# A vision tower of state-space tokens, gated scan and mixture of experts on one core: feature products over 128 rows, with their operands regrouped by transfers on the chip

## The reference

```python
K   = 2 * Re( sum_n Ct[c,h,n] * exp(dA_log[h,n] * l) )      # 16 x 256 x 512: the tokens
h   = concat(cls_tok, K)                                     # 16 x 257 x 512
u   = layernorm(layernorm(h)) * gamma + beta
a, b, c = split(u @ W_in + b_in);  s_t = (1 - sig(a)) s_{t-1} + sig(a) b
h  += (s * tanh(c)) @ W_out + b_out + layernorm(h) @ W_skip + b_skip
x   = layernorm(h)
h  += sum over the 2 best of 8 experts: score * (silu(x Wg) * (x Wu)) Wd
    + (silu(x Sg) * (x Su)) Sd                               # shared expert
```

## Time and profile before

| what | value |
|---|---|
| three runs | 1191.7, 1199.46 (median), 1201.67 us |
| profiled execution | 1196.48 us, its span 1194.8 us |
| mean granted TensorE clock | 0.944 of full |
| PE, DVE, ACT, POOL busy | 1059.5, 812.2, 347.2, 383.9 us (89, 68, 29, 32% of the span) |
| first stage, rounds 3 to 14 | 192.60 to 663.72 us |
| expert stage | from about 773 us |

### The profile page before, as it was taken

One profiled execution on the slowest core, in us unless ns is written; L12 is line 12 of the kernel. 1 busy time (PEld: TensorE's weight loads), 2 busy tenths in 40 slices (PEclk: granted clock), 3 DMA queues, 4 the chain that ended last, 5 costly groups with the idle time before them and its releaser, 6 DMA issues.

```text
span 1194.8 us, 26490 instructions
## 1 busy us (share of the span) xinstructions
PE 1059.5 (89%) x7869; PEld 696.9 (58%) x7870; DVE 812.2 (68%) x2123; ACT 347.2 (29%) x658; POOL 383.9 (32%) x352
## 2 busy tenths in 40 slices
PE   3046898999999999999999994989999999999995
PEld 3034566666766676667766771655555555555552
DVE  7976988898889888988898563544444444444442
ACT  4413433443344333443344332111111111111110
POOL 1011221222123211332022210145545656655554
PEclk8556998999999999999999997899999999999998
DMA  7322456455545555455535589689998777877885
GB/s 247 112 53 54 105 159 154 124 152 173 149 127 150 170 151 143 139 171 162 165 112 157 170 258 371 188 170 217 224 172 132 130 130 130 134 132 128 133 124 74
DMA packets 311150, 183.57 MB, mean 154 GB/s; under 512 B 261218, under 2 KB 280034, under 8 KB 309044
## 3 DMA queue, kind: packets, MB, share of 16 engines
q1 hardware_dynamic: 292948, 135.83, 46.8%
q0 software_dynamic: 15504, 36.46, 15.2%
q10 hardware_dynamic: 2640, 10.54, 2.3%
HBM read 53.40 MB, written 79.73 MB: 111 GB/s over the span
## 4 chain that ended last, share of the span: by engine, by line
PE 75%; DVE 3%; SPq 3%; DMA 3%; issue 2%; ACT 1%; POOLq 0%; POOL 0%; ACTq 0%; DVEq 0%
PE bank L997 30%; PE bank L1146 10%; PE bank L1156 10%; PE bank L1147 10%; PE bank L1072 8%; PE bank L1011 4%; DMA out<-x2w,rows_in 2%; SPq L779 1%; SPq L781 1%; PE bank L1076 1%; ACT tokens L1202 1%; PE bank L1062 1%; DMA wexp<-w_halves 1%; PE bank L1075 1%; DVE wexp L1351 0%
## 5 line engine op out<-in xcount | busy, mean ns | idle before, releaser
L997 PE MATMUL bank<-wexp 128*128 128x256 f16 (+2 forms) x3252 | 418.6, 291 | 24.8 <-issue 9.5
L997 PEld LDWEIGHTS bank<-wexp 128*128 128x128 f16 x3252 | 316.4, 101 | 110.7 <-issue 33.7
L1146 PE MATMUL bank<-wexp,rows_in 128*128 x852 | 255.5, 313 | 9.6 <-issue 6.9
L1147 PE MATMUL bank<-wexp,rows_in 128*128 x852 | 255.1, 312 | 0.0
L975 POOL DMA_INDIRECT out<-x2w,rows_in x71 | 113.7, 1601 | 116.0 <-DMA out<-x2w,rows_in 82.8
L927 POOL TENSOR_TENSOR inv<-var,power 128x4 f32<-128x4 f32 x17 | 29.2, 1717 | 375.0 <-DVE var L1533 375.0
L1689 DVE SCALAR_TENSOR_TENSOR mixed<-bank,mixed 128x352 f32<-128x352 f32 x71 | 37.2, 525 | 161.0 <-ACT mixed L1308 108.4
L963 POOL TENSOR_TENSOR ex<-base,ld 128x8 f32<-128x8 f32 x71 | 120.7, 1699 | 75.9 <-DVE ld L1668 56.0
L1146 PEld LDWEIGHTS bank<-wexp,rows_in 128*128 128x128 f16 x852 | 83.1, 98 | 66.6 <-issue 25.9
L1308 ACT ACTIVATE mixed<-bank 128x352 f32<-128x352 f32 x71 | 32.9, 464 | 295.3 <-PE bank L1147 295.3
L1156 PE MATMUL bank<-wexp,gates 128*128 (+1 forms) x477 | 111.7, 379 | 2.9 <-DVE x2w L1684 2.9
(11 more groups left out here) (281 smaller groups left out, 1247.3 us busy)
## 6 DMA issues: line engine op xcount, KB each, us to landing
w_halves<-rows_in SPq DMA_DIRECT2D x16, 704.0 KB
wexp<-w_halves ACTq DMA_DIRECT2D x1, 8704.0 KB
...
h_tok<-tokens SPq DMA_DIRECT2D x16, 512.0 KB, 2.7
...
```

The lines of the kernel that those rows point to most:

```text
L997: last = MM(dst, stat_of(step, a), mov_of(step, b), start=(s_ == 0 and a + b == 0), stop=(s_ == len(steps) - 1 and a == 1))
L1146: MM(GB[:, 0:H], xT[b][:, a, c, :], wexp[:, u, o:o + H], start=s_, stop=e_)
L1147: last = MM(UB[:, 0:H], xT[b][:, a, c, :], wexp[:, u, o + H:o + 2 * H], start=s_, stop=e_)
```

## The change

1. **Features.** After `tok_e` and after `tok_p`, SP copies the operands inside SBUF (`regroup`): half `f` of partition block `t` goes to partition block `f` of index `t`. `ea` goes to `et`, `pp` to `pt`, four DMAs each. PE then makes one product over all 128 partitions per `t` and `j`: 16 per chunk. `et` and `pt` are so read by PE, and `tok_e` part 0 waits for the previous feature products.
2. **Order on DVE.** `tok_e` for chunk k+2 moves from the end of body k-1 into body k, between the gate products; `tok_p` 1 to 5 stand around the second `project_out`, ahead of both `rows_lo` and both `down_out`.
3. **Banks.** The features use the banks of `shared_down` (3 and 0) instead of 1 and 2; PE waits for `c_dev` (`down_out`) instead of `c_gm` ahead of them, and for `c_toke` only ahead of the third gate product group.
4. **End of the first stage.** `pads_d` rows become whole rows (2112 bytes): SP writes their zeros at the end of body 1, and `pad_rows` is one copy from DRAM to DRAM per expert. Expert 4's copy stands ahead of the second x3 transpose of body 16. ACT's weight DMA is issued at the start of body 15. In the expert stage SP loads a unit at every third tile instead of every second.
5. **First rounds.** PE makes products whose result nobody reads (`idle_products`): 36 in body -1, 10 and 28 in body 0.

```diff
@@ -807,6 +807,12 @@
                     row = sp.value_load(tbl[0:1, 1, bass.ds(i, 1)], min_val=0, max_val=NR - P)
                     sp.dma_start_transpose(xT[b][:].rearrange("p h k t -> p (h k) t"), xs_d[bass.ds(row, P), 0:2 * D]).then_inc(d_xl[b], 16)
                     sp.dma_start(ext[b][:].bitcast(I32), xs_d[bass.ds(row, P), 2 * D:XW].bitcast(I32)).then_inc(d_xl[b], 16)
+
+                def regroup(to, of, sem):
+
+                    for t in range(2):
+                        for f in range(2):
+                            sp.dma_start(to[f * N:(f + 1) * N, t], of[t * N:(t + 1) * N, f]).then_inc(sem, 16)
 
                 def body(k, q):
                     if htok(k + 1):
@@ -819,6 +825,11 @@
                             sp.dma_start(hx[:, i, :].rearrange("p (b a) -> p b a", a=NA), src[:, i]).then_inc(c_hx, 16)
                     elif k + 1 == 0:
                         sp.dma_start(hx[:, 0, :], cls_tok.rearrange("a b d -> (a b) d").broadcast_to([P, D])).then_inc(c_hx, 32)
+                    if isinstance(k, int) and k == -1:
+                        sp.wait_ge(c_eap, 1)
+                        regroup(et, ea, c_ste)
+                        sp.wait_ge(c_tokp, 1)
+                        regroup(pt, pp, c_stp)
                     if htok(k - 1):
                         sp.wait_ge(c_wl, k - 1)
                         store_unit(k - 2)
...
                             load(b, b)
+                    if htok(k + 2) and not (isinstance(k, int) and k == -1):
+                        sp.wait_ge(c_eap, k + 2)
+                        regroup(et, ea, c_ste)
                     if has(k + 1):
                         n = k + 1
                         sp.wait_ge(c_lo2, n + 1)
@@ -853,13 +867,17 @@
                         at_least(sp, c_rt, n)
                         apart(sp, c_sps)
                         for i in range(tiles(n)):
+                            if i == 1 and isinstance(k, int) and k == NCH:
+                                pad_rows(sp, 4)
+                            if i == tiles(n) - 1 and htok(k + 2):
+                                sp.wait_ge(c_tokp, k + 2)
+                                regroup(pt, pp, c_stp)
                             sp.wait_ge(c_lo3, n * 2 + (i + 1) * 2 // tiles(n))
                             apart(sp, c_sps)
                             sp.dma_start_transpose(x3T[:, i].rearrange("p h k t -> p (h k) t"),
                                                    x3w[:, i, 0:2 * D]).then_inc(c_e3[i], 16)
                     if isinstance(k, int) and k == NCH:
-                        for e in range(4, 6):
-                            pad_rows(sp, e)
+                        pad_rows(sp, 5)
                     if has(k - 1):
...
                         sp.dma_start(dst, hst[:].rearrange("p j t a -> p (j t a)")).then_inc(c_hst, 16)
+                    if isinstance(k, int) and k == 1:
+                        for r in range(4):
+                            sp.dma_start(pads_d[:, r, :, 0:2 * D].bitcast(I32).rearrange("e q w -> q e w"),
+                                         zrow[:, 0:2 * D].bitcast(I32).rearrange("p (o w) -> p o w", o=1).broadcast_to([P, E, D])).then_inc(c_pw, 16)
                     if isinstance(k, int) and k == 2:
...
@@ -1001,17 +1023,15 @@
                 def features(k):
 
                     n = k + 2
-                    pe.wait_ge(c_tokp, n)
+                    pe.wait_ge(c_stp, n * 64)
+                    pe.wait_ge(c_ste, n * 64)
                     if not isinstance(k, int) or k >= 1:
-                        pe.wait_ge(c_gm, k * 6)
-                    for j in range(JC):
-                        for f in range(2):
-                            for t in range(2):
-                                q = slice(t * N, (t + 1) * N)
-                                last = MM(BU[t][:, j * NA:(j + 1) * NA], pp[q, f, j].rearrange("p b c -> p (b c)"),
-                                          ea[q, f, j, :], start=(f == 0), stop=(f == 1))
-                                if j == JC - 1 and f == 1:
-                                    last.then_inc(c_tokm, 1)
+                        pe.wait_ge(c_dev, k * 2)
+                    for t in range(2):
+                        for j in range(JC):
+                            last = MM(BU[t][:, j * NA:(j + 1) * NA], pt[:, t, j].rearrange("p b c -> p (b c)"),
+                                      et[:, t, j, :], start=True, stop=True)
+                        last.then_inc(c_tokm, 1)
 
                 def body(k, q):
 
...
 
+                    def idle_products(count):
+
+                        for i in range(count):
+                            MM(BD[0][:], ident16[:], wskip[:, 0, 0, :], start=True, stop=True)
+
                     if isinstance(k, int) and k == -1:
+                        idle_products(36)
                         features(k)
+                    if isinstance(k, int) and k == 0:
+                        pe.wait_ge(c_toke, 2)
+                        idle_products(10)
                     if has(k - 1):
                         early = 1 if isinstance(k, int) and k == LAST else 3 if isinstance(k, int) and k == NCH else 4
                         for m in range(early):
@@ -1109,6 +1138,8 @@
                         last.then_inc(c_gt, 1)
 
                     first_win = has(k + 1) and not (isinstance(k, int) and k == -1)
+                    if isinstance(k, int) and k == 0:
+                        idle_products(28)
                     if first_win:
                         input_project()
                     if htok(k + 2) and not (isinstance(k, int) and k == -1):
...
             row = eng.value_load(runi[0:1, e:e + 1], min_val=0, max_val=ZERO - 3 * P)
-            eng.dma_start(xs_d[bass.ds(row, 3 * P), 2 * D:XW].bitcast(I32),
-                          pads_d[e].rearrange("r q w -> (r q) w")[bass.ds(turn, 3 * P)]).then_inc(c_z, 16)
-            eng.dma_start(xs_d[bass.ds(row, 3 * P), 0:2 * D].bitcast(I32).rearrange("(i p) w -> p i w", p=P),
-                          zrow[:, 0:2 * D].bitcast(I32).rearrange("p (o w) -> p o w", o=1).broadcast_to([P, 3, D])).then_inc(c_z, 16)
+            eng.dma_start(xs_d[bass.ds(row, 3 * P), :], pads_d[e].rearrange("r q w -> (r q) w")[bass.ds(turn, 3 * P), :]).then_inc(c_z, 16)
 
...
@@ -1615,25 +1655,23 @@
                     if isinstance(k, int) and k == 2:
                         seats()
                     if tokens2:
+                        if shared:
+                            tok_p(k + 2, 1)
                         tok_p(k + 2, 2)
                     if has(k) and tiles(k) == 2:
                         project_out(1)
+                    if tokens2:
+                        tok_p(k + 2, 3)
+                        tok_p(k + 2, 4)
+                        tok_p(k + 2, 5)
                     if has(k):
                         rows_lo(k, 0)
-                    if tokens2:
-                        tok_p(k + 2, 3)
+                    if has(k) and tiles(k) == 2:
+                        rows_lo(k, 1)
                     if shared:
                         down_out(0)
-                    if tokens2:
-                        tok_p(k + 2, 4)
-                        tok_p(k + 2, 5)
-                    if has(k) and tiles(k) == 2:
-                        rows_lo(k, 1)
                     if shared and tiles(k - 1) == 2:
                         down_out(1)
-                    if htok(k + 3):
-                        for f in range(4):
-                            tok_e(k + 3, f)
                     if htok(k):
                         v.wait_ge(c_wh, k * 2 - 1)
                         for g in range(2):
```

53 lines of the change are left out of this document (32 added, 21 removed).

## The result

The changed kernel takes 1392.07 us (1390.21 to 1394.72, 4 runs) beside 1195.58 us for the kernel before on the same chip: ratio 1.1645, 95% interval 1.1602 to 1.1689. It is slower, by more than the range allowed. The profiled execution took 1393.54 us (span 1391.8), the mean granted clock fell from 0.944 to 0.884.

The account below looks back on a forecast made before the run. PE was taken to bound the rounds, DVE barely behind. Terms 59 + 36 + 7 + 18 + 2 + 4 - 10 - 1 = +115 us gave 1314 us from the 1199.46 median (chance 0.50); 8-in-10 range 1235 to 1345.

Parts of the forecast that it names:

- the circle: Loop: DVE completes operands, copies follow, then PE's features, behind which DVE's next products queue; round 43.6 instead of 38.68 us.
- PE's point T+5.9: Round's start T: DVE's second gate product waits for ACT, which waits for PE, until T+5.9; this stays.
- DVE's 27.0 us: Loop, DVE without a wait from T+5.9 to the end of `tok_p` part 5: 24.4 - 1.2 + 3.8, reaching T+32.9.
- `rows_lo(0)` and the transpose's issue: Loop, between `tok_p` and the copies: 0.6 us plus 1.2 us for the first x3 transpose, reaching T+34.7.
- The copies, 2.1 + 2.7 us: Loop, four 256 KB copies on SP: 2.1 us of issue, 2.7 of landing (upper bound 8.6), reaching T+39.5.
- The products, 3.3 us at full clock: Loop, PE's 32 feature products over 128 rows: 3.3 us instead of 3.79, bounds 1.9 and 3.9.
- The clock, +36 in all: Loop: a fall in each of rounds 3 to 14 (+13), features caught in half of 14 rounds (+23); bounds -7, +59.
- rival 1: Loop: clock falls inside the wait every round, all feature products at 1.2 GHz; 1337 us, chance 0.20.
- Rounds 3 to 14, +92: Twelve loop rounds at +4.9 us each, +59, with 33 of the clock's +36.
- Round 1, +7: Round 1, with gate products half as wide: 33.7 becomes 40.7 us, bounds 5 and 10.
- Round 2, +18: Round 2: `h_tok` loads behind the zero rows cost 12.5 us, plus 4.9 and the rest of a clock fall.
- Rounds -1 and 0, +2: First rounds: copies come 4 us after the operands, idle products stand in waits; +2 us, bounds -5 and +6.

Follow-up runs that it names:

- e2: Changed kernel with 30 more idle PE products in front of the features of every round from 1 on; 1332.99 us, ratio 1.1115.
- e13: Changed kernel with two of the four copies of `pp` (imaginary half) left out in rounds 0 to 14; 1363.27 us, ratio 1.1385.
- e10: Changed kernel with two of the four `pp` copies issued on ACT's queue and two on SP's; 1393.61 us, ratio 1.1644.
- e1: Kernel before with everything of the change except the feature part; 1212.74 us, ratio 1.0104.
- e5: e1 with one of the four 2 MB zero-row transfers in each of rounds 0 to 3; 1196.30 us, ratio 0.9978.
- e9: e5 with the first eight expert weight blocks sent in two halves, in ACT's bodies 15 and 16; 1187.91 us, ratio 0.9926.
- e6: e5 with ACT's expert weight transfer back at the end of body 15, as in the kernel before; 1192.29 us, ratio 0.9953.
- e3: Changed kernel with the four `pp` copies issued ahead of both x3 transposes; 1372.98 us, ratio 1.1462.
- e4: Changed kernel with `tok_e` moved to the end of the body before, behind `scan`; 1358.06 us, ratio 1.1338.
- e8: Changed kernel with operands prepared and copied a round ahead, features between second and third gate product, banks 3 and 5; 1286.49 us, ratio 1.0769.
- e7: Changed kernel with the edits of e2 (here 14 idle products), e3 and e4 together; 1276.70 us, ratio 1.0701.
- e11: e8 with 9 idle products between the router products, zero rows spread and expert weights in two halves; 1263.16 us, ratio 1.0556.

## Why the prediction was wrong, step by step

Direction, place and the circle were right (slower, 0.87), the size was not: +115 us forecast, +197 measured, outside the range to 1345. Two steps failed in the loop: the four copies were given 4.8 us and took 7.35, and the clock was taken to catch the features in half of the rounds and caught them in all. Of the 82 us that are missing, rounds 3 to 14 carry 51; the rest is rounds 15 (11.5), 2 (10), -1 and 0 (8) and 1 (4), less 2 in the stage of experts, where the forecast's line for the clock is shared out over rounds 1 to 14.

- **PE's point T+5.9**: T+7.35. The first products of the round run at the lower clock; e2 shows it.
- **DVE's 27.0 us**: 26.5 (507.68 to 534.16). Right. `rows_lo(0)` and the transpose's issue: 2.07 for 1.8. Right.
- **The copies, 2.1 + 2.7 us**: 7.35. This term was mis-sized, and in the loop it is the largest part of the miss. An issue is 0.87 us, not the 0.52 of the earlier trace rows, and landing was taken from the h_tok store, 2.7 us, where a copy needs 4.3. The upper bound (8.6) covered it, the value taken did not. +2.6 us a round, 31 us in rounds 3 to 14; e13 shows that the term shrinks with the number of copies, e10 that a second queue does not shrink it.
- **The products, 3.3 us at full clock, bounds 1.9 and 3.9**: 3.79 at full clock (120.79), exactly the time of the 64 half-height products, and 7.09 at the lower, again the same. The bounds held. The rule of the Trainium skill that stood beside the sum, TensorEngine Tiling (Array Packing), section Key Properties, by which row tiles can work in parallel, so that the halves had already run side by side and nothing is saved, fits the trace: the two times are equal. The float32 rows of 175 and 244 ns that I argued with misled only by a little; those products are other shapes.
- **The clock, +36 in all, a half of the rounds caught**: the second step that failed, in the share of the rounds and not in the price of a fall. It fell in the wait in every round from 1 to 14, features and the next round's start both paid, and e2 puts 59 us on it, by the profiled executions 57 of them in rounds 3 to 14; that is 17 us more there than the forecast had, with the four falls of before counted. A fall in every round was rival 1, with a chance of 0.20, and its place, the wait itself. I had taken it from a kernel whose rounds hold no such wait, where the clock fell in a third of the rounds behind small products; a wait of 7 us is not the same evidence. e2's 59 is not the same quantity as this term's upper bound of +59: it holds the four falls of before as well, some 7 us, so the clock added some 52.
- **Rounds 3 to 14, +92 (59, and 33 of the 36)**: +142.6. Of the 50.8 us of the round read above, 7.3 are over the forecast's 43.6: clock 4.7, copies 2.6, products 0.3, DVE -0.5, the rest 0.2; of the clock's part the forecast had put 2.7 in its own line for the clock, and 0.5 is in the 39.3 of before. So of the 51 us by which these rounds exceed the forecast, the copies carry some 31 and the clock some 17.
- **Round 1, +7**: +12.3, the same two terms. **Round 2, +18**: +29.5. The wait for `h_tok` was foreseen at 12.5 us for the zero rows; statistics stood at T+28.7 (199.44) and not at the forecast's T+23 (T+10.5 before), and e1 and e5 price the zero rows at 16 to 18 us. The rest is the circle's surplus.
- **Rounds -1 and 0, +2**: +10.1. The four copies of `ea` and the four of `pp` stand open here, one behind the other: features at 81.40 instead of 73.25. I had counted 4 us for it.
- **Round 15, +4, bounds 0 and 8**: +15.5. The place was wrong, not only the size: I looked at the x3 transposes, and it was the h_tok store and loads at the round's start that stood behind the weights (e1: the round is 14 us longer there too, without any circle; with the weights in two halves, e9, it is still 5 us longer, with 4.24 us of wait for an x2 transpose).
- **Round 16, -10**: -9.9. Right in size; but its reason was half right. Of the two, the earlier weights did it (e6), the pad copies did nothing measurable.
- **Expert stage, -1**: -3.1, too little to explain.

The rivals: the second (cheap products, quick copies) and the third (copies covered) fall with the rows of the copies. For the third to hold, DVE's chain would have had to lose what e3, e4 and e8 together take out of the circle, and even e7 and e11, with idle products, stay at 41.7 us and more against 38.7. No version with copies came under the kernel before. What the change had to win, PE time for the products, was nothing.
